# Global attention of layer 2: scores held by query and turned tile by tile, or made by key with nothing turned

## The reference

```
s     = gated, normalised x                     # 256 x 3136
theta = theta_w s + theta_b                     # 128 x 3136, queries
phi   = phi_w s + phi_b                         # 128 x 3136, keys
g     = g_w s + g_b                             # 128 x 3136, values
attn  = softmax over j of (theta_i . phi_j)     # 3136 x 3136
nl_i  = sum over j of attn_ij g_j
x     = x + s + out_w nl + out_b
```

## Time and profile before

| | us |
|---|---|
| median of 3 runs (7061.96 to 7073.7) | 7062.63 |
| the profiled execution | 7086.07 |
| its span in the trace | 7084.3 |
| TensorE's mean granted clock in it | 0.959 of full |
| PE busy in the span | 6159.0 (87%) |
| DVE busy | 6069.4 (86%) |
| ACT busy | 5648.1 (80%) |
| POOL busy | 5317.2 (75%) |

### The profile page before, as it was taken

How to read it: one execution, slowest core, us unless ns; L and a number is a source line. 1 busy time by engine, 2 the same in 40 slices (tenths; PEclk the granted TensorE clock), 3 DMA queues, 4 the chain that set the end, 5 groups by cost and what they waited for, 6 DMA issues and landing times. The chain is left out here.

```text
span 7084.3 us, 132922 instructions
## 1 busy us (share of the span) xinstructions
PE 6159.0 (87%) x38014; PEld 4202.7 (59%) x38014; DVE 6069.4 (86%) x10800; ACT 5648.1 (80%) x8200; POOL 5317.2 (75%) x2595
## 2 busy tenths in 40 slices
PE   6778899987888888888888888888888888888888
PEld 4546676764555555555555555555555555555556
DVE  5453454454999999999999999999999999999998
ACT  5472232324999999999999999999999999999998
POOL 4361000004999999999999999999999999999997
PEclk8787999998999999999999999999999999999999
DMA  3221000002000000000000000100000000000000
GB/s 98 67 70 44 1 0 0 0 0 66 11 1 1 1 1 1 1 12 1 1 1 1 1 1 2 29 1 1 1 1 1 1 2 1 4 4 4 4 4 6
DMA packets 110733, 79.81 MB, mean 11 GB/s; under 512 B 68490, under 2 KB 108290, under 8 KB 109826
## 3 DMA queue, kind: packets, MB, share of 16 engines
q1 hardware_dynamic: 107306, 77.71, 3.8%
q10 hardware_dynamic: 3288, 0.33, 0.0%
HBM read 48.70 MB, written 22.86 MB: 10 GB/s over the span
## 5 line engine op out<-in xcount | busy, mean ns | idle before, releaser
L1609 POOL TENSOR_TENSOR a_s<-a_s,a_v 128x1568 f32<-128x1568 f32 x784 | 2766.4, 3529 | 321.3 <-ACT a_s L1820 299.9
L1645 PE MATMUL a_right_sides<-a_s,diag_d 128*128 128x392 f32 x6272 | 2294.1, 510 | 4.2 <-POOL a_s L1609 4.2
L1745 DVE SCALAR_TENSOR_TENSOR a_kan<-a_s,spline_c,a_kan 128x784 f32<-128x784 f32 x1568 | 1616.4, 1031 | 0.6
L1645 PEld LDWEIGHTS a_right_sides<-a_s,diag_d 128*128 128x128 f32 x6272 | 1167.3, 196 | 722.0 <-issue 71.7
L1602 POOL TENSOR_TENSOR a_inner<-a_inner,a_x 128x784 f32<-128x784 f32 x784 | 1456.6, 1858 | 65.4
L1811 ACT ACTIVATE a_v<-a_a 128x784 f32<-128x784 f32 x1568 | 1335.0, 852 | 0.3
L1667 PEld LDWEIGHTS a_weighed<-a_V,a_probT 128*128 128x128 f32 x9800 | 1237.7, 192 | 162.0
L1667 PE MATMUL a_weighed<-a_V,a_probT 128*128 128x65 f32 x9800 | 1228.2, 269 | 0.0
L1820 ACT ACTIVATE a_s<-a_v 128x1568 f32<-128x1568 f32 x784 | 1186.4, 1513 | 5.0
L1632 PE MATMUL a_scores<-a_K,a_q 32*64 32x392 f32 x6272 | 699.7, 515 | 426.2 <-DVE a_kan L1727 409.4
L1714 DVE TENSOR_SCALAR a_x<-a_scores 128x196 f32<-128x196 f32 (+1 forms) x2352 | 995.1, 423 | 20.3 <-PE a_scores L1632 20.3
(11 more groups left out here) (199 smaller groups left out, 5271.6 us busy)
## 6 DMA issues: line engine op xcount, KB each, us to landing
rows<-bias_rows_dram SPq DMA_DIRECT2D x112, 91.0 KB
ve<-v_dram SPq DMA_DIRECT2D x98, 104.0 KB
X<-in_x_dram SPq DMA_DIRECT2D x4, 1568.0 KB, 13.9
xn<-kt SPq DMA_DIRECT2D x56, 112.0 KB, 2.2
v_dram<-vt SPq DMA_DIRECT2D x56, 112.0 KB, 2.0
a_q<-q_dram SPq DMA_DIRECT2D x392, 16.0 KB
mask<-in_window_mask_dram SPq DMA_DIRECT2D x56, 98.0 KB, 1.9
a_V<-v_dram SPq DMA_DIRECT2D x4, 812.5 KB, 8.5
```

The source lines that it names most:

```text
L1609: eng.tensor_tensor(both, both, v[g % 2][:, :, :].rearrange("p j c -> p (j c)"), ALU.mult).then_inc(cubed, 1)
L1645: mm = eng.matmul(up[:, j, 0:SUB], steps[i][:, :], s[g][:, i, SUB * j:SUB * (j + 1)], start=(i == 0), stop=(i == 1))
L1745: eng.scalar_tensor_tensor(F, banked(s[g][:, j, :]), c[:, 3 + j:4 + j], F, ALU.mult, ALU.add).then_inc(left_added, 1)
```

## The change

Scores are made by key: a key tile's 128 keys lie on the partitions, and 448 queries (a block, QB) on the free dimension. There are 7 blocks of 25 key tiles, 175 tiles in all, numbered n. One step of the new order, s, handles up to four different tiles on the engines:

- PE: by_key(s) makes tile s (448 columns) into one of three PSUM banks; values(s - 32) multiplies gT with tile s - 32.
- ACT: keep(s) copies tile s to SBUF, into one of 35 buffers; then exponent(s - 29), in place.
- DVE: raise_high(s) takes the elementwise maximum of tile s with the block's running maximum (high); then take_limit(s - 29) subtracts the block's limit from tile s - 29, in place.
- POOL: adds tile n, once exponentiated, to the block's running sum (acc).

When a block's 25 tiles are made, its running maximum is turned by four transposes (turn_high), reduced along the free dimension, laid out as diagonals (share_max) and spread to all partitions by one matmul with ones (spread_max), which gives the limit of each query on every partition. The sum over the keys is a matmul of acc with a column of ones (sum_keys), inverted, spread in the same way (share_inverse, spread_inverse) and multiplied with the weighed values into nl (divide). The probabilities themselves are not turned any more. The loops are written out in full instead of running as hardware loops.

```
-    SUB2 = L // 8
-    CH = KEY_TILES2 // 2 + 1
...
+    QB, QT2 = CHUNK, TILE
+    BLOCKS = CHUNKS
+    TILES_MADE = BLOCKS * KEY_TILES2
+    TAKE, WEIGH, RING = KEY_TILES2 + 4, KEY_TILES2 + 7, 35
+    TURN_MAX, SPREAD_MAX, SUM, SPREAD_SUM, DIVIDE = 0, 2, 6, 8, 10
+    STEPS = KEY_TILES2 * (BLOCKS + 1) + DIVIDE + 1
...
             @block.gpsimd
...
+                for n in range(TILES_MADE):
+                    pool.wait_ge(exp_done, n + 1)
+                    if n:
+                        pool.wait_ge(acc_done, n)
...
+                        pool.tensor_tensor(acc[j % 2][low:P, :], acc[j % 2][low:P, :], prob[n % RING][low:P, :], ALU.add).then_inc(acc_done, 1)
...
             @block.tensor
...
+                def by_key(n):
+                    j, k = n // KEY_TILES2, n % KEY_TILES2
+                    if n >= 3:
+                        pe.wait_ge(t_kept, n - 2)
+                    pe.matmul(tp[n % 3][:, 0:QB], phi[:, first_key(k):first_key(k) + P], theta[:, QB * j:QB * (j + 1)], start=True, stop=True).then_inc(t_made, 1)
...
+                def values(n):
+                    pe.wait_ge(exp_done, n + 1)
...
+                    pe.matmul(op[j % 2][:, 0:QB], gT[:, k, :], prob[n % RING][:, :], start=(k == 0), stop=(k == KEY_TILES2 - 1)).then_inc(weighed, 1)
...
+                for s in range(STEPS):
+                    if s < TILES_MADE:
+                        by_key(s)
...
+                    if 0 <= s - WEIGH < TILES_MADE:
+                        values(s - WEIGH)
...
             @block.vector
...
+                def raise_high(n):
+                    dve.wait_ge(t_kept, n + 1)
...
+                        dve.wait_ge(maxed, n)
+                        dve.tensor_tensor(high[j % 2][:, :], prob[n % RING][:, :], high[j % 2][:, :], ALU.max).then_inc(maxed, 1)
...
+                def take_limit(n):
+                    if k == 0:
+                        dve.wait_ge(limit_kept, j + 1)
+                    dve.tensor_tensor(prob[n % RING][:, :], prob[n % RING][:, :], limit[j % 2][:, :], ALU.subtract).then_inc(d_taken, 1)
...
+                for s in range(STEPS):
+                    if s < TILES_MADE:
+                        raise_high(s)
+                    if behind(s, TURN_MAX, 1) is not None:
+                        share_max(behind(s, TURN_MAX, 1))
+                    if behind(s, SUM, 2) is not None:
+                        share_inverse(behind(s, SUM, 2))
+                    if 0 <= s - TAKE < TILES_MADE:
+                        take_limit(s - TAKE)
+                    if behind(s, DIVIDE, 2) is not None:
+                        divide(behind(s, DIVIDE, 2))
...
             @block.scalar
...
+                def keep(n):
+                    act.wait_ge(t_made, n + 1)
+                    if n >= RING:
+                        act.wait_ge(weighed, n - RING + 1)
+                        act.wait_ge(acc_done, n - RING + 1)
+                    act.copy(prob[n % RING][:, :], tp[n % 3][:, 0:QB]).then_inc(t_kept, 1)
...
+                def exponent(n):
+                    act.wait_ge(d_taken, n + 1)
+                    act.activation(prob[n % RING][:, :], prob[n % RING][:, :], ACT.Exp).then_inc(exp_done, 1)
...
+                for s in range(STEPS):
+                    if s < TILES_MADE:
+                        keep(s)
...
+                    if 0 <= s - TAKE < TILES_MADE:
+                        exponent(s - TAKE)
```

More of the change, by code:

```diff
@@ L1178, in copied @@
[L1178 to L1185, removed]
+        prob = [sb(f"prob{r}", [P, QB]) for r in range(RING)]
@@ new lines, in softmax2 @@
+        high = [sb(f"high{r}", [P, QB]) for r in range(2)]
+        limit = [sb(f"limit{r}", [P, QB]) for r in range(2)]
+        acc = [sb(f"acc{r}", [P, QB]) for r in range(2)]
+        inv = sb("inv", [P, QB])
+        ones = sb("ones", [P, P])
+        rmax, rinv = sb("rmax", [QT2, 4]), sb("rinv", [QT2, 4])
+        share_m, share_i = sb("share_m", [QT2, 4, QT2]), sb("share_i", [QT2, 4, QT2])
+        tp = [ps(f"by_key{r}", [P, 512]) for r in range(3)]
+        op = [ps(f"op{r}", [P, 512]) for r in range(2)]
@@ new lines, in softmax2 @@
+        hp = ps("turned", [QT2, 4, P])
+        spread = ps("spread", [P, 512])
+        sums = ps("sums", [QT2, 4])
+        ones_set, t_made, maxed, t_kept, high_turned, max_step, max_shared, max_spread, limit_kept, d_taken, exp_done, acc_done, weighed, summed, inverted, inv_shared, inv_spread, inv_kept, o_placed = (
+            sem(n) for n in ("ones_set", "t_made", "maxed", "t_kept", "high_turned", "max_step", "max_shared", "max_spread", "limit_kept", "d_taken", "exp_done", "acc_done", "weighed", "summed", "inverted", "inv_shared",
+                             "inv_spread", "inv_kept", "o_placed"))
@@ L1187, in softmax2, with behind @@
+        def behind(s, at, blocks):
+            j, k = s // KEY_TILES2 - blocks, s % KEY_TILES2
+            return j if k == at and 0 <= j < BLOCKS else None
+        diagonal = m.ident[0:QT2, 0:QT2].unsqueeze(1).to_broadcast([QT2, 4, QT2])
+        flat = lambda share: share[:, :, :].rearrange("p t q -> p (t q)")
         with nc.Block() as block:
@@ L1211, in values @@
[L1211 to L1228, removed]
@@ L1240, in _, with turn_high @@
-                pipeline(pe, TURNS2, [(scores, 0), (spread_shares, 2), (values, 1)])
+                def by_key(n):
+                    j, k = n // KEY_TILES2, n % KEY_TILES2
+                    if n >= 3:
+                        pe.wait_ge(t_kept, n - 2)
+                    pe.matmul(tp[n % 3][:, 0:QB], phi[:, first_key(k):first_key(k) + P], theta[:, QB * j:QB * (j + 1)], start=True, stop=True).then_inc(t_made, 1)
+                def turn_high(j):
+                    pe.wait_ge(maxed, KEY_TILES2 * (j + 1))
+                    if j:
+                        pe.wait_ge(max_step, j)
+                    for t in range(4):
+                        mm = pe.transpose(hp[:, t, :], high[j % 2][:, QT2 * t:QT2 * (t + 1)], m.ident[:, :])
+                    mm.then_inc(high_turned, 1)
@@ new lines, in spread_max @@
+                def spread_max(j):
+                    pe.wait_ge(max_shared, j + 1)
+                    if j:
+                        pe.wait_ge(limit_kept, j)
+                    if j >= 2:
+                        pe.wait_ge(inv_kept, j - 1)
+                    pe.matmul(spread[:, 0:QB], ones[0:QT2, :], flat(share_m), start=True, stop=True).then_inc(max_spread, 1)
+                def values(n):
+                    j, k = n // KEY_TILES2, n % KEY_TILES2
+                    pe.wait_ge(exp_done, n + 1)
+                    if k == 0 and j >= 2:
+                        pe.wait_ge(o_placed, j - 1)
+                    pe.matmul(op[j % 2][:, 0:QB], gT[:, k, :], prob[n % RING][:, :], start=(k == 0), stop=(k == KEY_TILES2 - 1)).then_inc(weighed, 1)
@@ new lines, in sum_keys, with spread_inverse @@
+                def sum_keys(j):
+                    pe.wait_ge(acc_done, KEY_TILES2 * (j + 1))
+                    if j:
+                        pe.wait_ge(inverted, j)
+                    for t in range(4):
+                        mm = pe.matmul(sums[:, t:t + 1], acc[j % 2][:, QT2 * t:QT2 * (t + 1)], ones[:, 0:1], start=True, stop=True)
+                    mm.then_inc(summed, 1)
+                def spread_inverse(j):
+                    pe.wait_ge(inv_shared, j + 1)
+                    pe.wait_ge(limit_kept, min(j + 2, BLOCKS))
+                    if j:
+                        pe.wait_ge(inv_kept, j)
+                    pe.matmul(spread[:, 0:QB], ones[0:QT2, :], flat(share_i), start=True, stop=True).then_inc(inv_spread, 1)
@@ L1256, in normalise @@
[L1256 to L1262, removed]
@@ new lines, in share_inverse, with divide @@
+                def share_inverse(j):
+                    dve.wait_ge(summed, j + 1)
+                    dve.reciprocal(rinv[:, :], sums[:, :]).then_inc(inverted, 1)
+                    dve.wait_ge(inverted, j + 1)
+                    if j:
+                        dve.wait_ge(inv_spread, j)
+                    dve.tensor_tensor(share_i[:, :, :], diagonal, rinv[:, :].unsqueeze(2).to_broadcast([QT2, 4, QT2]), ALU.mult).then_inc(inv_shared, 1)
+                def divide(j):
+                    dve.wait_ge(inv_kept, j + 1)
+                    dve.wait_ge(weighed, KEY_TILES2 * (j + 1))
+                    dve.tensor_tensor(nl[:, QB * j:QB * (j + 1)], op[j % 2][:, 0:QB], inv[:, :], ALU.mult).then_inc(o_placed, 1)
@@ L1278, in _ @@
+                dve.wait_ge(o_placed, BLOCKS)
             @block.scalar
             def _(act):
-                def copies(eng, u, r):
-                    for c in range(0, CH, 2):
-                        copy_chunk(eng, eng.copy, u, r, c, copied_a)
-                def exponent(eng, u, r):
-                    for h in range(halves(u)):
-                        eng.wait_ge(max_ready, 2 * u + h + 1)
-                        eng.activation(prob[r][h][:, :], prob[r][h][:, :], ACT.Exp, bias=nmax[r][:, h:h + 1],
```

(26 more changed lines are left out.)

95 lines of the change are left out of this document (26 added, 69 removed).

## The result

The changed kernel takes **7342.4 us**, the median of 4 runs (7335.2 to 7347.46), against 7064.68 us of the kernel before beside it: a recorded ratio of 1.0383, 95% interval [1.0371, 1.0396] (the two medians alone give 1.0393). It is slower by 278 us; 7408 had been forecast, in a range of 7140 to 7490.

A forecast was written before the change was run, and what follows sets the result against it. PE was taken to bound softmax2 before; after, waits among ACT, DVE and POOL make 2.97 us rounds. Per sample 25 + 434 + 12 + 57 = 528 us against 355.7, +345 for both: 7408 us on the median, range 7140 to 7490.

The forecast's parts named there:

- PE sets the stage before: Softmax2: PE busy about 348 of 354.50 us per sample; its work falls to about 283, gained only if PE sets the pace.
- The tie: Softmax2 rounds: ACT and DVE wait for each other within one step, so durations add to 2.24 us against PE's 1.50.
- The hold: Softmax2 rounds: DVE's two-SBUF maximum waits until POOL's addition ends, 0.73 us, making a round 2.97 us.
- rows 7: Profile rows before the change: beside a POOL memset ending at 58.17, a DVE instruction on 128x2 took 5.51 us, ending at 58.19.
- the upper end: Maximum's wait for POOL's addition, put between 0 and 0.73 us: 0.73 was taken.
- the 0.08 us from ACT to POOL: Hand-over in a softmax2 round: POOL's addition starts 0.08 us after ACT's exponent ends.
- Block extras: Reduction, reciprocal and diagonals on DVE between maximum and subtraction: 1.98 us per block, six times, 12 us per sample.
- Steps 0 to 28: Start of a softmax2 sample, tiles only made, kept and maximised: PE sets them, 25 us.
- The last part: End of a softmax2 sample: last 29 subtractions and additions exclude each other, 53 us, plus 4 for the finish: 57 us.
- Rival 1: Softmax2 rounds: no exclusion between DVE and POOL, 2.24 us per round, 7158 us in all; chance 0.20.
- Rival 2: Softmax2 rounds: PE's clock falls to the lower level, a tile with extras takes 3.22 us, 7481 us; chance 0.08.
- Rival 3: Softmax2: PE stays the bound, rounds under 1.92 us, a sample takes 300 us, -111 us, 6952 us; chance 0.06.

The follow-up runs named there:

- e7: e6 with the limit also kept in PSUM, so the subtraction has one SBUF tensor: 6972.4 us, 0.9853 of the kernel before.
- e1: Changed kernel with POOL's addition replaced by a memset of 128x1152 into its own tile, key sums left out: 7174.6 us, 1.0147 of the kernel before.
- e5: Changed kernel with the maximum reading its new tile from the PSUM bank instead of SBUF, order kept: 7207.5 us, 1.0194 of the kernel before.
- e3: Changed kernel with DVE's subtraction of tile s - 29 put ahead of the maximum of tile s: 7125.7 us, 1.0078 of the kernel before.
- e6: Changed kernel with the edits of e3 and e5 together: 6993.5 us, 0.9875 of the kernel before.
- e2: Changed kernel with POOL's addition replaced by an in-place multiplication of its own 128x1152 tile, sums left out: 7968.0 us, 1.1273 of the kernel before.

## Why the prediction was right

- **PE sets the stage before, and what PE saves counts only if it goes on setting the pace**: right. 65 us per sample of PE's work went (348 to 283 by the prediction's sum; in e7's first sample PE is busy for 287.6), and the change got nothing of it; e7, with the same PE work, did.
- **The tie**: right, and in size. 2.24 us were worked out for the round without a hold; 2.25 (first tile of a block), 2.22 (e1) and 2.30 (e5) were measured. Cutting it alone gave 217 us (e3).
- **The hold**: right in kind, mis-sized. The forecast had the maximum wait for the whole addition and then take its full 0.62, 0.73 us in all. It ends 0.48 us after the addition, so some 0.14 us of its own time pass during the wait: hold 0.61, round 2.83 for 2.97. That is 0.14 x 146 x 2 = 41 us of the 66 by which 7408 was too high. The row it leaned on was a poorer witness than it was taken for: in rows 7 a memset held DVE, and in e1 a memset holds no maximum. The two-tensor form is held by reads, which no row of before showed, so as far as that row goes the choice of the upper end was luck. So was the 0.08 us from ACT to POOL: the wait in its row is put down to DVE; here it is 0.07 (902.84 to 902.91).
- **Block extras**: 12 us were allowed per sample, for six blocks, but by the program's steps only five of each kind (steps 50 to 150 and 56 to 156) fall into the rounds. The two rounds with extras measure 1.03 and 0.75 us over the others (1.98 allowed), and the first tile's short round gives 0.58 back in each block, which the sum left out: 1.20 net, 6 us for five. By the stretch it is 416 - 145 x 2.83 = 6.
- **Steps 0 to 28**: 25 us expected, 26.2 measured, on PE as said. **The last part**: 57 expected, 54.3 measured, by errors that nearly cancel. One subtraction and one addition take 1.49 us (23 additions in 34.29) and not 1.84, so 29 of them are 43 us, not 53; the rest, the last sums, inversions, spread and division, is 11 us, not 4 (6.1 of it behind the last addition).
- **Rival 1** (no exclusion, 7158) fell with the maximum at 1.23 us; e1, which leaves out just that, ran at 7174.6. **Rival 2** (PE's clock): the clock did fall, to a mean of 0.93, with passes 0.75 us apart (the lower level) after PE had idled 5.58 us before a turn. Four such passes take 3.00 us, more than a round, but the stretches were short and no keep of the rounds stood idle for by_key, as the 0.0 us of the row below says, so it wasn't on the path. **Rival 3** (PE stays the bound, faster, 6952) was wrong for this order; its condition, rounds under 1.92 us, came true in e6 and e7, and so did its gain: 111 us were worked out, e7 has 107 (6972.4 against 7079.07).

The keeps of the first sample's rounds, 819 to 1235 us (count, busy us, mean ns of one, idle time before):

```profile
L1320 ACT COPY a_prob<-a_by_key 128x448 f32<-128x448 f32 x145 | 74.4, 513 | 0.0
```

The terms by sample, expected and measured: 25 and 26.2, 446 and 416, 57 and 54.3; 528 and 496.5.

The Trainium skill (SBUF — State Buffer, "Who interferes with whom") says that a VectorE instruction with two SBUF inputs contends with a GpSimd one that reads SBUF and not with one that only writes. The traces agree on both halves (1.23 against 0.62 us), and, for the maximum (e5, e7) and the subtraction (e7), on its rule that one SBUF input is free of it outside VectorE's 2-port modes, in which it also uses the ports shared with GpSimd. Its rule that the later one is blocked until the earlier is through would have given the 2.97 us; the measured 2.83 decides. The difference is the 0.14 us of the maximum's own time that pass during the wait; which part of the instruction that is, no run shows.

## What to carry to other kernels

When two engines hand work to each other twice within one step, write down both programs' order before adding up loads: if each waits for the other's instruction of the same step, their durations add, however many tiles lie between the data; putting the instruction with the older data first costs nothing and gave 217 us here. Beside a POOL that reads SBUF, give DVE one operand in PSUM, and make a term for the hold where that can't be. Taking work off the bounding engine gains only where the round that the other engines then make is shown to be shorter than what that engine took before: 2.83 us of round here lost, 1.5 in e7 won.

## What the runs showed of the hardware

- A held DVE instruction has part of its own time behind it when it is let go: the maximum ends 0.48 us after the addition, where it takes 0.62 when free (the change). After a POOL operation on one tensor it ended 0.24 us behind the recorded end (e2).
- Which DVE forms a POOL memset holds: the two-tensor maximum not (0.62 us). A copy from SBUF to SBUF yes, on the same 448 columns and beside the same memset (e1): 0.91 us, where it takes 0.39 with POOL idle (least, median and most ns of the 14 copies below).

```profile
1039.88 0.91 DVE L1269 COPY a_high<-a_prob 128x448 f32<-128x448 f32 x1 [1.06 <-ACT a_prob L1321]
L1269 DVE COPY a_high<-a_prob x14: 394/905/908, 795.5 to 1561.8; 128x448 f32<-128x448 f32 x14
```

- The hold goes both ways: where DVE's instruction was first, POOL's addition took 1.38 us instead of 1.13 (e3, at 906.05, behind a subtraction begun at 905.82; it is the first of the two merged above).
- POOL's multiplication of 128x1152 by a constant, in place, took 3.12 us, 2.7 ns per column, more than its two-tensor addition (1.13 us for 448, 2.5 ns), and as long with DVE idle (e2). The cause stays open.
